# Two transformer layers on one core: the token parts of the delta rule's front made for all chunks while the membranes run, and kept in DRAM

## The chip, the cores and the metric

The kernel runs on one core of a Trainium2 chip. The metric is the device time of one execution in microseconds (us). Before the change the median of three runs is 1696.33 us (1694.0 to 1699.62). The profile comes from one execution of its own, which took 1701.06 us; its span, from the first to the last instruction, is 1699.3 us. Engines are named PE (TensorE, matmuls), PEld (its weight loads), ACT (ScalarE), DVE (VectorE), POOL (GpSimd) and SP (SyncE, which here only issues DMAs).

## The reference, cut to what matters

The input x is one sequence of 2048 tokens of width 128. The first layer normalises and modulates x and then runs a gated delta rule whose gates depend on spikes. Only this part is touched:

```
h = silu(causal_conv(rms(x)))                         # [T, 128]
q, k = unit(h @ Wq), unit(h @ Wk)                     # 8 heads of 64, each divided by its norm + 1e-6
v = h @ Wv
drive = h @ Wspike
alpha_base = silu(h @ Wau + bau) @ Wad + bad
beta_base  = h @ Wbeta + bbeta
for each token t:
    mem   = 0.9 * mem + drive[t]
    spike = mem > 0.5 ;  mem = mem - 0.5 * spike
    alpha = sigmoid(alpha_base[t] + asp * spike)      # 1 where a head has no spike
    beta  = sigmoid(beta_base[t] + sum(spike * bsp))  # 0 where a head has no spike
    s = alpha * s                                     # s: 64 x 64 per head
    s = s + (beta * k[t]) outer (v[t] - k[t] @ s)
    out[t] = q[t] @ s
```

q, k, v, alpha_base and beta_base depend on the token alone. The spikes need the membrane recurrence, and alpha, beta and the state need the spikes. After this come an output projection with a gate, a gated feed forward net, and a second layer; nothing of those is changed.

## The kernel before, in words

All data are float32. The 2048 tokens are 16 chunks (NT) of 128 (P); 8 heads are 4 pairs (NP). Four phases follow one another, each one block of code in which every engine has its own written order of instructions and waits on semaphores of the others. A phase ends when all its engines have ended. The count of a semaphore is worked out from lists of step names (`Steps`): `at(name, i)` is that step of round i, `before(name, i)` the same step one round earlier.

1. `setup_phase` (lines 76 to 329) loads weights, makes h (called `hh`, features on partitions) and the drive.
2. `spike_phase` (332 to 409) runs the membranes. DVE goes through 128 token positions, for all chunks side by side, with four small instructions for each (lines 378, 381, 383 and 385, two halves of 32 columns), and repeats the whole pass at least three times, until the states at the chunks' borders agree. Beside it PE turns x and h in 32 transposes (357) and ACT copies them back (365). Both are then done with the phase.
3. `delta_phase` (412 to 1203) works chunk by chunk. Its *back* is the delta rule of chunk i: products within blocks of 8 tokens (`base`, 767), products of neighbouring blocks of 8, 16, 32 and 64 (`blocks`, 795; the two heads of a pair stand in different halves of the rows), a row by row inversion on DVE (1102, 1107) that starts from a spread made by PE (787) and copied by ACT (618), a table `tt` (1123), transposes of it (806), four rounds of `join` (823, 834, 836, then 844, 850), and the state (858 to 888). Its *front* prepares chunk i + 1 and is woven between: projections `k`, `q`, `v`, `au` and `drive_a`, norms (sums over a head by a matmul with `bd`, then four ACT instructions and a product on DVE), the gates (`zb`, whose first half is alpha's and second beta's exponent), their running sum `G`, exponentials of its differences (`EX`, ACT line 588), and scaled copies of k and q (1033, 1039, 1047). Chunks 0 to 14 run in hardware loops; chunk 15 stands by itself, with no front.
4. `post_phase` does the rest, from about 1205 us on.

PE's order in a chunk is: `base`, `front_au` (of i + 1), `blocks`, `front_sums` (i + 1: 4 matmuls for `drive_a`, 2 of 512 columns for the norms, 8 for beta), `transposed`, `join` 8, `front_count` (i + 1, 512 columns), `join` 16 and 32, `last_join`, `state1`, `solve`, `front_late` (v of i + 1), `seen_by_q`, `front_k` and `front_q` (of i + 2), `state2`. Each matmul of this program is two MATMUL records in the trace.

DVE's order is: `front_spikes` (967, and 969 for au), `base`, `front_au` (974, 976, 978), `blocks` with `tt`, `front_z`, `front_sums`, the joins with `front_active` and `front_exponents` between them, `rest`, `front_unit`, `keep` (1152), `front_upper`, `update` (1157), `front_late`.

POOL squares k and q (511), multiplies spikes (513), and scales beta k (517, 521).

Of the kernel before, what the change touches and what calls it, by code (L numbers as in the profile page):

```python
# [19 lines left out]
P = 128  # L20
# [55 lines left out]
def setup_phase(nc, m, a):  # L76


    with ExitStack() as ctx:
# [164 lines left out]
        def _(eng):  # L244
            eng.memset(m.eps[:, 0:1], 1e-5)
            eng.memset(m.eps[:, 1:2], 1e-6).then_inc(vector_done, vec.one("eps"))
# [84 lines left out]

def spike_phase(nc, m):
# [6 lines left out]
    with ExitStack() as ctx:  # L339
# [9 lines left out]
        turned = ctx.enter_context(nc.semaphore("rows_turned"))  # L349
        columns = ctx.enter_context(nc.semaphore("columns_kept"))  # L350

        @block.tensor
        def _(eng):
            for k in range(8):
                src = (m.x, m.h)[k // 4]
                for n in range(4):
                    ins = eng.transpose(m.ps[:, k, P * n:P * n + P], src[:, 4 * (k % 4) + n, :], m.ident[:, :])
                ins.then_inc(turned, 1)

        @block.scalar  # L360
        def _(eng):
            for k in range(8):
                dst = (m.x, m.h)[k // 4]
                eng.wait_ge(turned, k + 1)
                eng.activation(dst[:, 4 * (k % 4):4 * (k % 4) + 4, :].rearrange("p n d -> p (n d)"), m.ps[:, k, :], ACT.Copy).then_inc(columns, 1)
# [46 lines left out]
def delta_phase(nc, m):  # L412
# [11 lines left out]
    with ExitStack() as ctx:  # L424
# [17 lines left out]
            "tensor_front": "k q au drive_a ksum qsum beta count v",  # L442
            "scalar_front": "hh k q au_e zb_e zb_ln beta_e n_ln n_rt n_ln2 n_rec lift_p lift_n v lift_up lift_all last",
            "vector_front": "spikes au0 au1 au2 au z b1 guard zfloor b0 active log_a G mid"
            + "".join(f" lo{s} hi{s}" for s in UPPER) + " toend unit b3 beta_k kq_base"
            + "".join(f" kq{s}" for s in UPPER) + " kq_all k_end",
            "pool_front": "square push km_base" + "".join(f" km{s}" for s in UPPER),
# [10 lines left out]
        beta_bias = ctx.enter_context(nc.semaphore("beta_bias"))  # L458
# [8 lines left out]
        square = m.arena[:, 4608:5632]  # L467
# [34 lines left out]

        @block.gpsimd
        def _(eng):
            eng.sem_inc(pool_front, fpool.credit)

            def front(n):

                eng.wait_ge(scalar_front, fact.at("q", n))
                eng.wait_ge(tensor_front, fpe.before("qsum", n))  # L510
                eng.tensor_tensor(square, kqf, kqf, ALU.mult).then_inc(pool_front, fpool.one("square"))
# [20 lines left out]
        def _(eng):  # L532
# [4 lines left out]
            def front_tokens(n):  # L537
                eng.wait_ge(tensor_front, fpe.before("v", n))
                eng.activation(m.hh_tile[:, :], m.hh[:, tok(n)], ACT.Copy).then_inc(scalar_front, fact.one("hh"))

            def front_kq(n):
                eng.wait_ge(tensor_front, fpe.at("k", n))
                eng.wait_ge(vector_front, fvec.before("kq_all", n))
                eng.wait_ge(pool_front, fpool.before("square", n))
                eng.activation(kq[:, 0, :], m.ps[:, 4, :], ACT.Copy).then_inc(scalar_front, fact.one("k"))
                eng.wait_ge(tensor_front, fpe.at("q", n))
                eng.activation(kq[:, 1, :], m.ps[:, 5, :], ACT.Copy).then_inc(scalar_front, fact.one("q"))  # L547

            def front_au(n):
                eng.wait_ge(vector_front, fvec.at("au0", n))  # L550
                eng.activation(m.au_e[:, :], m.au_x[:, :], ACT.Exp, scale=-1.0).then_inc(scalar_front, fact.one("au_e"))

# [11 lines left out]

            def front_norm1(n):

                eng.wait_ge(vector_front, fvec.at("guard", n))
                eng.activation(m.norm[:, :], m.norm[:, :], ACT.Ln).then_inc(scalar_front, fact.one("n_ln"))

            def front_norm2(n):  # L570
                eng.wait_ge(scalar_front, fact.at("n_ln", n))
                eng.activation(m.norm[:, :], m.norm[:, :], ACT.Exp, scale=0.5).then_inc(scalar_front, fact.one("n_rt"))

            def front_norm3(n):
                eng.wait_ge(scalar_front, fact.at("n_rt", n))
                eng.activation(m.norm[:, :], m.norm[:, :], ACT.Ln, bias=m.eps[:, 1:2]).then_inc(scalar_front, fact.one("n_ln2"))
                eng.wait_ge(scalar_front, fact.at("n_ln2", n))
                eng.activation(m.norm[:, :], m.norm[:, :], ACT.Exp, scale=-1.0).then_inc(scalar_front, fact.one("n_rec"))
# [17 lines left out]

            def front_v(n):
                eng.wait_ge(tensor_front, fpe.at("v", n))
                eng.wait_ge(vector_back, vec.before("rest", n))
                eng.activation(m.v[:, :], m.ps[:, 3, :], ACT.Copy).then_inc(scalar_front, fact.one("v"))  # L600
# [59 lines left out]
            front_tokens(0)  # L660
            front_kq(0)
            front_au(0)
            front_gates(0)
# [1531 lines left out]
```

## Time and profile before

| what | value |
|---|---|
| median of three runs | 1696.33 us (1694.0 to 1699.62) |
| profiled execution, its span | 1701.06 us, 1699.3 us |
| PE, PEld, DVE, ACT, POOL busy | 1178.4, 902.6, 1103.5, 601.2, 198.3 us |
| mean granted TensorE clock | 0.795 |
| membranes (first to last pass) | 96.5 to 284.7 us |
| delta rule, 16 chunks | 290 to 1204 us |
| DMA over the span | 7.22 MB, mean 4 GB/s |

Times within a phase are us from the span's start. The granted clock is a share: 1.00 is 2.4 GHz and 0.50 is 1.2 GHz, the only two levels in this trace. The engines overlap, so their busy times do not add up to the span; what a change is worth is to be read in its own phase.

### The profile page before, as it was taken

What the parts mean: (1) busy time and instruction counts of PE and PEld (TensorE: products, weight loads), DVE (VectorE), ACT (ScalarE), POOL (GpSimd) and SP (SyncE); (2) the same over time, 40 slices, a digit from 0 to 9 for tenths busy, and PEclk for the clock granted to TensorE, in tenths of its full rate; (3) what the DMA queues carried; (4) which work ended last, traced back from release to release, by engine and by line L of the source; (5) the groups of instructions that cost most, each with busy time, mean ns of one, the idle gap of its engine ahead of it and who ended that gap; (6) DMA issues with size and microseconds to landing.
All of it is one profiled execution on the core that took longest, in us unless ns stands there. A gap on an engine that the chain in (4) does not pass through costs nothing. (4 is left out here: it accounts for less than half of the span.)

```text
span 1699.3 us, 25028 instructions
## 1 busy us (share of the span) xinstructions
PE 1178.4 (69%) x8364; PEld 902.6 (53%) x8364; DVE 1103.5 (65%) x3471; ACT 601.2 (35%) x935; POOL 198.3 (12%) x189
## 2 busy tenths in 40 slices
PE   1230001488888988898888988889666879688786
PEld 1110001377777877787777876779423526346272
DVE  4788988777887778877797777872133325343251
ACT  3120000333444334443444534441325355363422
POOL 2000001301211012110211102110010102001000
PEclk8575555688899889898988999895578788886966
DMA  2000000000000000000000000000200000000000
GB/s 72 0 1 1 1 1 1 1 1 0 0 0 0 0 0 0 0 0 0 0 0 0 0 0 0 0 1 1 58 0 1 0 0 8 0 7 1 0 8 6
DMA packets 9746, 7.22 MB, mean 4 GB/s; under 512 B 3158, under 2 KB 7831, under 8 KB 9690
## 3 DMA queue, kind: packets, MB, share of 16 engines
q1 hardware_dynamic: 8170, 5.07, 1.1%
q10 hardware_dynamic: 1520, 1.48, 0.3%
q8 instruction: 25, 0.41, 0.1%
q14 instruction: 31, 0.25, 0.1%
HBM read 5.50 MB, written 1.05 MB: 4 GB/s over the span
## 5 line engine op out<-in xcount | busy, mean ns | idle before, releaser
L1133 DVE TENSOR_TENSOR delta_tm<-delta_tm,ps 128x256 f32<-128x256 f32 x96 | 40.4, 421 | 156.7 <-PE ps L836 156.7
L795 PE MATMUL ps<-delta_kq_up,delta_arena 64*128 64x128 f32 x1024 | 111.2, 400 | 37.2 <-ACT delta_kq L547 36.5
L795 PEld LDWEIGHTS ps<-delta_kq_up,delta_arena 64*128 64x128 f32 x1024 | 102.4, 302 | 62.2 <-ACT delta_kq L547 37.4
L893 PE MATMUL ps<-ones,beta_b 1*128 1x1 f32 x8 | 1.8, 346 | 190.9 <-PEq L339 190.9
L633 ACT ACTIVATE delta_xf<-ps 128x256 f32<-128x256 f32 (+1 forms) x128 | 48.9, 382 | 204.5 <-PE ps L823 140.2
L517 POOL TENSOR_TENSOR delta_km<-delta_beta_k,delta_arena 128x512 f32<-128x512 f32 x16 | 32.6, 2037 | 635.9 <-DVE delta_beta_k L1030 635.9
L834 PE MATMUL ps<-delta_xf,delta_tt 128*128 128x64 f32 x768 | 106.6, 284 | 0.0
L836 PE MATMUL ps<-delta_tt,delta_xf 128*128 128x64 f32 x768 | 106.6, 284 | 0.0
L823 PEld LDWEIGHTS ps<-delta_tm,drive 128*128 128x128 f32 x768 | 95.6, 201 | 17.0 <-DVE delta_zb L984 9.1
L893 PEld LDWEIGHTS ps<-ones,beta_b 1*128 1x128 f32 x8 | 1.8, 322 | 191.1 <-issue 191.1
L823 PE MATMUL ps<-delta_tm,drive 128*128 128x64 f32 x768 | 98.5, 284 | 6.1 <-ACT delta_tm L623 6.1
L834 PEld LDWEIGHTS ps<-delta_xf,delta_tt 128*128 128x128 f32 x768 | 98.6, 201 | 0.0
L836 PEld LDWEIGHTS ps<-delta_tt,delta_xf 128*128 128x128 f32 x768 | 98.6, 201 | 0.0
L378 DVE SCALAR_TENSOR_TENSOR kept<-mem 128x32 f32<-128x32 f32 x384 | 73.3, 191 | 12.3 <-remote 11.2
L1039 DVE TENSOR_TENSOR delta_kq_up<-delta_kq,delta_arena 128x256 f32<-128x256 f32 x128 | 75.8, 651 | 1.4
L383 DVE SCALAR_TENSOR_TENSOR mem<-kept,drive 128x32 f32<-128x32 f32 x384 | 73.3, 191 | 0.0
L385 DVE SCALAR_TENSOR_TENSOR mem<-kept,drive 128x32 f32<-128x32 f32 x384 | 71.7, 187 | 0.0
L381 DVE SCALAR_TENSOR_TENSOR kept<-mem 128x32 f32<-128x32 f32 x384 | 71.6, 187 | 0.0
L533 ACT ACT_TABLE_LOAD x1 | 1.3, 1283 | 189.5 <-PEq L339 189.5
L521 POOL TENSOR_TENSOR delta_arena<-delta_beta_k,delta_arena 128x256 f32<-128x256 f32 x64 | 57.2, 923 | 6.3 <-ACT delta_arena L588 6.3
L787 PE MATMUL ps<-drive,delta_block_ones 128*128 128x512 f32 x32 | 29.3, 1015 | 39.4 <-DVE drive L1070 37.4
L767 PE MATMUL ps<-delta_kq_base,delta_km 64*128 64x256 f32 x256 | 37.7, 417 | 25.2 <-DVE delta_state L1157 14.2
(372 smaller groups left out, 2923.1 us busy)
## 6 DMA issues: line engine op xcount, KB each, us to landing
out<-post_rows SPq DMA_DIRECT2D x4, 256.0 KB, 2.3
setup_wmod<-in_L_wmod ACTq DMA_DIRECT2D x2, 384.0 KB, 3.4
post_wff<-in_L_attn_Wff SPq DMA_DIRECT2D x3, 256.0 KB
post_w<-in_L_ffn_w SPq DMA_DIRECT2D x2, 256.0 KB
post_fc_q<-in_L_ffn_fc_q SPq DMA_DIRECT2D x2, 256.0 KB
setup_wspike<-in_L_attn_Wspike ACTq DMA_DIRECT2D x1, 256.0 KB
wq<-in_L_attn_Wq ACTq DMA_DIRECT2D x1, 256.0 KB
wk<-in_L_attn_Wk SPq DMA_DIRECT2D x1, 256.0 KB
```

Source lines behind the costliest of these rows:

```text
L378: eng.scalar_tensor_tensor(m.kept[:, a_half], u[:, t, a_half], 1.0, u[:, t, a_half], ALU.is_gt, ALU.subtract).then_inc(step_a, 1)
L381: eng.scalar_tensor_tensor(m.kept[:, b_half], u[:, t, b_half], 1.0, u[:, t, b_half], ALU.is_gt, ALU.subtract).then_inc(step_b, 1)
L383: eng.scalar_tensor_tensor(u[:, t + 1, a_half], m.kept[:, a_half], -DECAY, d[:, t, a_half], ALU.mult, ALU.add).then_inc(step_a, 1)
L385: eng.scalar_tensor_tensor(u[:, t + 1, b_half], m.kept[:, b_half], -DECAY, d[:, t, b_half], ALU.mult, ALU.add).then_inc(step_b, 1)
L521: eng.tensor_tensor(lo, halves(m.beta_k[:, :], s)[:, :, 0, :], lo, ALU.mult).then_inc(pool_front, fpool.one(f"km{s}"))
L633: eng.activation(dst, src, ACT.Copy).then_inc(scalar_back, act.one(f"X{s}{x}"))
L795: ins = eng.matmul(m.ps[:, at + h % 2, P * (h // 2):P * (h // 2) + P], up_lift[s][ks, cs], m.kq_up[s][ks, :, half], start=True, stop=True)
L823: ins = eng.matmul(m.ps[:, 4 + n, HD * (h % 4):HD * (h % 4) + HD], bt[s][:, h, :], cols(m.tm[:, h, :], 0), start=True, stop=True)
L834: eng.matmul(m.ps[:, 6 + n, HD * (h % 4):HD * (h % 4) + HD], m.tt[:, h, :], cols(m.xf[:, h, :], 0), start=True, stop=True)
L836: ins = eng.matmul(m.ps[:, 6 + n, 256 + HD * (h % 4):256 + HD * (h % 4) + HD], m.xf[:, h, :], cols(m.tt[:, h, :], 1), start=True, stop=True)
L1039: ins = eng.tensor_tensor(m.kq_up[s][:, a, :].rearrange("p (b s) -> p b s", s=s), halves(kq[:, a, :], s)[:, :, 1, :], halves(up_lift[s], s ...
L1133: eng.tensor_tensor(v, v, m.ps[:, 6 + n, 0:256].rearrange("p (b s) -> p b s", s=s), ALU.subtract).then_inc(vector_back, vec.one(f"TX{x}{s}"))
```

## The change

`prepare`, called in the spike phase in place of the bare transposes, makes k, q (with their norms), v, alpha_base and beta_base of all 16 chunks in 4 groups of 512 tokens and writes them to three DRAM tensors. PE has 28 matmuls of 512 columns for a group, ACT 13 instructions of 2048 columns and 4 of 512, POOL two products of 2048 columns, and SP five stores of 1 MB. Before them stand the old transposes and copies, the biases, and au of all tokens (4 matmuls; ACT copy, Exp, Ln, Exp; two POOL instructions). SP ends the phase by waiting for all stores.

In the delta phase SP loads each chunk's `zb`, `kq` and `v` into the same single buffers as before, each as soon as chunk i's last reader is done. The steps `hh`, `k`, `q`, `au_e`, the four norms and `v` leave ACT; `k`, `q`, `au`, `drive_a`, `ksum`, `qsum`, `v` and half of `beta` leave PE; `au0`, `au1`, `au2`, `au`, `guard` and `unit` leave DVE; `square` leaves POOL. With them go the waits on those steps. `front_z` and `b1` now add to what was loaded.

```diff
+def prepare(nc, ctx, m, block):          # called by spike_phase
+    @block.tensor
...
+        def projected(g, which, w, b):
+            for c in range(NP):
+                ins = eng.matmul(m.ps[:, 4 * b + c, :], w[:, c * P:c * P + P], m.hh[:, group(g)], start=True, stop=True)
...
+        for g in range(NG):
+            eng.wait_ge(scalar_made, act_at("b", g - 1) if g else act0.at("turn7"))
+            projected(g, "k", m.wk, 0)
+            eng.wait_ge(scalar_made, act_at("q_ln", g - 1) if g else act0.at("au"))
...         # v, then ksum, q, z, qsum, b
+    @block.scalar
...
+        for g in range(NG):
+            kept(g, "k", 0)              # copy, Square
...         # v copy
+            normed(g, "k", 0)            # Ln, Exp, Ln, Exp
+            kept(g, "q", 1)
...         # z copy, four b
+            normed(g, "q", 1)
+    @block.gpsimd
+        eng.memset(m.au[R:R + 1, :], 1.0).then_inc(pool_made, pool0.one("ones"))
+        eng.wait_ge(scalar_made, act0.at("au"))
+        eng.tensor_scalar(m.au[0:R, :], m.au[0:R, :], FLOOR, None, ALU.max).then_inc(pool_made, pool0.one("floor"))
+        eng.wait_ge(scalar_made, act0.at("au_sig"))
+        eng.tensor_tensor(m.au[0:R, :], m.au[0:R, :], m.au_e[:, :], ALU.mult).then_inc(pool_made, pool0.one("silu"))
+        for g in range(NG):
+            for a, which in enumerate("kq"):
+                eng.wait_ge(scalar_made, act_at(f"{which}_rec", g))
...
+                eng.tensor_tensor(by_chunk(m.unit[:, a, :]), by_block(m.raw[:, a, :]), by_block(m.norms[:, :]), ALU.mult).then_inc(pool_made, pool.one(which))
...
+        @block.sync                      # delta phase
+            def scores_and_gates(n):
+                if n:
+                    eng.wait_ge(vector_front, fvec.at("G", n - 1))
+                    eng.wait_ge(scalar_front, fact.at("beta_e", n - 1))
+                eng.dma_start(zb[:, :, :], m.zb_store[n]).then_inc(zb_in, 16)
...         # values(n) after "rest", keys_and_queries(n) after "kq_all" of chunk n - 1
         def chunk(i):
             base(i)
             eng.wait_ge(scalar_back, act.before("out", i))
-            front_au(i + 1)
-            blocks(i, True)
-            front_sums(i + 1)
+            blocks(i)
+            front_beta(i + 1)            # 4 matmuls of 128 columns
             transposed(i)
             join(i, 8)
             front_count(i + 1)
...
             solve(i)
-            front_late(i + 1)
             seen_by_q(i)
-            if not last:
-                eng.wait_ge(scalar_back, act.at("kend", i))
-                front_k(i + 2)
             eng.wait_ge(scalar_back, act.at("solved", i))
-            if not last:
-                front_q(i + 2)
             state2(i)
```

## Rows read from the trace of the kernel before

**Rows 1.** The page: busy time of the engines, and granted clock in 40 slices.
```profile
PE 1178.4 (69%) x8364; PEld 902.6 (53%) x8364; DVE 1103.5 (65%) x3471; ACT 601.2 (35%) x935; POOL 198.3 (12%) x189
PEclk8575555688899889898988999895578788886966
```

**Rows 2.** Windows: stretch, length, busy PE, PEld, DVE, ACT, POOL, clock, DMA share, GB/s.
```profile
96.50:284.70 188.20, 2.91 (x27) 2.67 (x25) 176.38 (x1551) 3.92 (x8) 0.00 (x0) 0.52 0.00 1
709.90:712.30 2.40, 0.08 (x1) 0.00 (x0) 2.40 (x5) 1.07 (x2) 0.00 (x0) 0.69 0.00 0
718.10:723.90 5.80, 5.77 (x35) 4.04 (x35) 5.46 (x20) 1.67 (x5) 0.00 (x0) 0.50 0.00 0
723.90:728.50 4.60, 4.60 (x29) 3.64 (x28) 4.19 (x15) 0.65 (x2) 0.00 (x0) 0.94 0.00 0
728.10:754.90 26.80, 25.94 (x230) 24.86 (x229) 16.68 (x35) 12.88 (x23) 0.00 (x0) 1.00 0.00 0
758.70:781.80 23.10, 17.41 (x145) 13.21 (x144) 22.18 (x63) 6.75 (x16) 6.48 (x6) 0.78 0.00 0
```

**Rows 3.** Windows of chunk 15, which has no front.
```profile
1145.00:1150.80 5.80, 5.76 (x34) 3.99 (x34) 4.13 (x20) 1.67 (x5) 0.00 (x0) 0.50 0.00 0
1150.80:1154.10 3.30, 0.00 (x0) 0.00 (x0) 3.16 (x10) 0.65 (x2) 0.00 (x0) 0.95 0.00 0
1154.10:1200.00 45.90, 45.83 (x222) 45.03 (x224) 5.66 (x15) 5.64 (x14) 0.00 (x0) 0.50 0.00 1
```

**Rows 4.** Timeline of a middle chunk: start, us, engine, line, operation.
```profile
712.14 0.33 DVE L969 TENSOR_SCALAR delta_au_x<-ps,bau 64x128 f32<-64x128 f32 x1
718.13 2.07 PE L787 MATMUL ps<-drive,delta_block_ones 128*128 128x512 f32 x2 [1.98 <-DVE drive L1070]
720.24 0.60 ACT L618 ACTIVATE drive<-ps 128x512 f32<-128x512 f32 x1 [7.43 <-PE ps L787]
726.88 1.23 DVE L1123 TENSOR_TENSOR delta_tt<-drive,delta_block_of 128x1024 f32<-128x1024 f32 x1
735.48 1.08 PE L746 MATMUL ps<-delta_spk,bd 128*128 128x512 f32 x2
752.86 1.99 PE L869 MATMUL ps<-drive,delta_tt 128*128 128x64 f32 x16 [0.44 <-DVE drive L1146]
754.89 0.60 ACT L650 ACTIVATE delta_u_rows<-ps 128x512 f32<-128x512 f32 x1
756.38 2.33 ACT L588 ACTIVATE delta_arena<-delta_arena 128x2560 f32<-128x2560 f32 x1
```

**Rows 5.** Timeline of chunk 15.
```profile
1147.74 0.17 DVE L1102 TENSOR_TENSOR drive<-drive 128x8 f32<-128x8 f32 x1 [1.53 <-ACT drive L618]
1152.89 1.22 DVE L1123 TENSOR_TENSOR delta_tt<-drive,delta_block_of 128x1024 f32<-128x1024 f32 x1
1196.25 3.68 PE L869 MATMUL ps<-drive,delta_tt 128*128 128x64 f32 x16
```

**Rows 6.** Lines 1152 and 181: count, duration ns min/median/max, first and last start.
```profile
L1152 DVE TENSOR_TENSOR delta_state<-delta_state,delta_last x16: 426/1499/1516, 382.5 to 1201.9; 128x256 f32<-128x256 f32 x16
L181 ACT ACTIVATE setup_arena<-setup_arena x1: 1909/1909/1909, 14.2 to 14.2; 128x2048 f32<-128x2048 f32 x1
```

**Rows 7.** Timeline of POOL and DVE.
```profile
712.48 1.89 POOL L511 TENSOR_TENSOR delta_arena<-delta_kq 128x1024 f32<-128x1024 f32 x1 [3.80 <-ACT delta_kq L547]
756.33 2.03 POOL L517 TENSOR_TENSOR delta_km<-delta_beta_k,delta_arena 128x512 f32<-128x512 f32 x1 [40.96 <-DVE delta_beta_k L1030]
757.14 1.50 DVE L1152 TENSOR_TENSOR delta_state<-delta_state,delta_last 128x256 f32<-128x256 f32 x1
766.18 1.89 POOL L511 TENSOR_TENSOR delta_arena<-delta_kq 128x1024 f32<-128x1024 f32 x1 [3.80 <-ACT delta_kq L547]
```

**Rows 8.** Timeline of the first chunk's front.
```profile
315.35 1.06 ACT L556 ACTIVATE delta_zb<-delta_zb 128x1024 f32<-128x1024 f32 x1 [12.43 <-DVE delta_zb L990]
323.89 2.32 ACT L588 ACTIVATE delta_arena<-delta_arena 128x2560 f32<-128x2560 f32 x1
```

More of the change, by code:

```diff
@@ L329, in _, with prepare_tensors, sb @@
                                           2.0, None, ALU.mult).then_inc(vector_done, vec.one(f"drive{n}"))
+def prepare_tensors(nc, ctx, m):
+    def sb(name, shape, dt=F32):
+        return ctx.enter_context(nc.sbuf_tensor("prep_" + name, shape, dt))
+    m.raw = sb("raw", [P, 2, 2048]); m.squares = sb("squares", [P, 2048]); m.norms = sb("norms", [P, 2048])
+    m.unit = sb("unit", [P, 2, 2048]); m.v_rows = sb("v_rows", [P, 2048]); m.zb_cols = sb("zb_cols", [P, 2, 2048])
+    m.au = sb("au", [R + 1, T]); m.au_e = sb("au_e", [R, T]); m.beta_bias = sb("beta_bias", [P, NP])
@@ L348, in spike_phase @@
         a_half, b_half = slice(0, W), slice(W, 2 * W)
[L349 to L365, printed above, removed]
+        prepare(nc, ctx, m, block)
         @block.vector
@@ L441, in delta_phase @@
             + " rest keep update",
[L442 to L445, printed above, removed]
+            "tensor_front": "beta count",
+            "scalar_front": "zb_e zb_ln beta_e lift_p lift_n lift_up lift_all last",
+            "vector_front": "spikes z b1 zfloor b0 active log_a G mid"
+            + "".join(f" lo{s} hi{s}" for s in UPPER) + " toend b3 beta_k kq_base"
             + "".join(f" kq{s}" for s in UPPER) + " kq_all k_end",
-            "pool_front": "square push km_base" + "".join(f" km{s}" for s in UPPER),
+            "pool_front": "push km_base" + "".join(f" km{s}" for s in UPPER),
         }
@@ L535, in _ @@
             eng.sem_inc(scalar_back, act.credit)
[L537 to L551, printed above, removed]
             def front_gates(n):
@@ L713, in head, with front_beta @@
                 return slice(HD * (h % 2), HD * (h % 2) + HD), slice(P * (h // 2), P * (h // 2) + P)
-            def project(bank, w, rhs, rows=P):
+            def front_beta(n):
+                eng.wait_ge(vector_front, fvec.at("spikes", n))
+                eng.wait_ge(vector_back, vec.before("up8b", n))
                 for c in range(NP):
-                    ins = eng.matmul(m.ps[:, bank, c * P:c * P + P], w[:, c * P:c * P + P], rhs, start=True, stop=True)
-                return ins
-            def front_k(n):
-                project(4, m.wk, m.hh[:, tok(n)]).then_inc(tensor_front, fpe.one("k"))
@@ L769, in base, with blocks @@
                                 ins.then_inc(tensor_back, pe.one(f"base{n + e}"))
-            def blocks(i, ahead):
+            def blocks(i):
                 for s in UPPER:
@@ L830, in join @@
                         eng.wait_ge(vector_back, vec.at(f"up16{x}", i))
-                        if ahead:
-                            eng.wait_ge(vector_front, fvec.at("guard", i + 1))
                     for h in range(4 * n, 4 * n + 4):
@@ L890, in state2, with chunk @@
                 ins.then_inc(tensor_back, pe.one("update"))
[L892 to L905 removed]
+            front_beta(0)
+            front_count(0)
+            def chunk(i):
                 base(i)
                 eng.wait_ge(scalar_back, act.before("out", i))
[L909 to L911 removed]
+                blocks(i)
+                front_beta(i + 1)
                 transposed(i)
```

283 lines of the change are left out of this document (176 added, 107 removed).

## The prediction

> **What bounds the kernel now.** I read the page first, then windows by stretch, then the timeline of one middle chunk and of the last one. The page shows PE and DVE both near two thirds, and a granted clock that is low in slices 4 to 8 and again after the delta rule [rows 1]. The windows tell why. While the membranes run (96.5 to 284.7) DVE has 1551 instructions and PE, ACT and POOL have next to nothing [rows 2]: this is the free room the change wants. In the delta rule line 511 comes once a chunk, at 712.48 and at 766.18 [rows 7]: a chunk has a period of 53.7 us.
>
> I cut that period at three points. (A) From the end of `tt` on DVE (726.88 + 1.23 = 728.1) to the end of the solve on PE (752.86 + 1.99 = 754.85): 26.8 us, PE busy 25.9, clock 1.00. (B) From there to the end of ACT's 2560-column Exp (756.38 + 2.33 = 758.7): 3.9 us. (C) From there to the next end of `tt` (781.8): 23.1 us, DVE busy 22.2 [rows 2, 4]. So A is PE's, B is ACT's, C is DVE's, and work is worth something only where it stands on its own engine's stretch.
>
> **What leaves the loop.** Most of it is covered. On DVE the three au steps (974 to 978) are 1.4 us, but they lie under the spread: PE 2.07 and ACT 0.60 us, after which the rows may start at 720.84 [rows 4]. Chunk 15 has no au steps, and there DVE waits 1.53 us for that same copy [rows 5]. So they are worth 0. Line 969 stands in C and is worth its step of 0.3. `unit` and the four norms are on DVE and ACT in A, where PE is the bound: 0 there. In B, after the solve, ACT copies u_rows, then v (waiting for PE's v), then starts the Exp at 756.38, 0.9 after the copy of u_rows ends at 755.49; with the v step gone that 0.9 goes. On PE `front_sums` fills 723.9 to 728.5, which DVE's `tt` makes it wait for anyway until 728.1: 0.3 or so, and 0.2 more at the first join. The sum is 0.3 + 0.9 + 0.5 = 1.7 us a chunk, 15 times: 25 us, if the clock stays as it is. Bounds: 0.9 (only B) to 3 a chunk.
>
> The first chunk's front is serial and gains more. Its gates wait for au, two sums and the guard; ACT's first Exp, after 12.4 us of idle, starts at 315.35 and the 2560-column one at 323.89 [rows 8]. Without au, sums (two 512-column matmuls at half clock) and squares the first Exp can start some 11 us earlier, and the norms no longer stand between it and the last. I take 12 us (bounds 8 to 16).
>
> **What the loads cost.** Each chunk loads 1.3 MB in three transfers, each started when the chunk before has done with the buffer. Three new waits stand on DVE: on `zb` in `front_z` (behind it b1, for which PE's first join waits), on `kq` before beta k (behind it line 1033, `keep`, and PE's next `base`), on v in `rest` (behind it the solve). By the order of the code each load has most of a chunk between its start and that wait, and SP has nothing else in its queue. I take 0, with bounds of 0 and 1 us a chunk, covered by the 53.7 us of the chunk itself.
>
> **What goes under the membranes.** ACT's wide instruction is 1.91 us [rows 6], so a group of 512 tokens costs it 13 x 1.91 + 4 x 0.6 = 27 us, plus waits for ksum and for qsum and b. Four 512-column matmuls are 3.4 us at full clock, 6.8 at half (the pair of line 787 takes 2.07 at 0.50, that of line 746 1.08 at 1.00 [rows 4], about 0.2 of each being pipeline). That makes 36 to 45 us a group, 144 to 180 for four. Transposes, au and its three Exp/Ln take some 25 ahead, the last product and store some 9 behind: 178 to 214 from 96, an end at 274 to 310. The membranes end at 284.7 now.
>
> But POOL does not run beside DVE for nothing. Line 1152 reads two operands from SBUF; in chunk 15, with POOL idle, it takes 0.43 us, in the 15 others 1.50, and it ends at 758.64, right after POOL's line 517 ends at 758.36 [rows 6, 7]. DVE was held until POOL's instruction was over. Lines 378 to 385 also read two operands from SBUF, and a pass is a chain of them. POOL gets 8 products of 2048 columns; at line 511's 1.89 us for 1024 [rows 7] that is 3.8 us each, 30 us, and two more of 2048 columns for au, 8 us. If each stops the chain for its length, the membranes take 38 us more, end at 323, and hide the whole preparation. No row shows this form held, so the bounds are 0 (not held; then the late end of the preparation costs 0 to 25 instead) and 45. I take 38, nearest to line 1152.
>
> The Trainium skill, page "SBUF — State Buffer", section "SBUF: two separate sides", calls the pair of ports that DVE and POOL share an exclusive lock, held for a whole instruction, which a DVE instruction with two SBUF inputs needs when POOL reads SBUF too. By that rule the term is the full 38. Where the trace can be read (line 1152), it agrees.
>
> **What happens to TensorE's clock.** This decides the sign. Chunk 15 is the delta rule with no front, so it is a preview. There PE stands idle from 1150.8 to 1154.1, the clock falls to 0.50, and stays there from 1154.1 to 1200.0 although PE is busy 45.83 of 45.90 us [rows 3]. The joins, 64-column matmuls each behind a weight load, do not bring it back. Stretch A takes from 1154.1 to 1196.25 + 3.68 = 1199.9 there [rows 5]: 45.8 us in place of 26.8, with less in it.
>
> In a middle chunk the clock also falls, at about 711 after a short idle (0.69 in 709.9 to 712.3), and is 0.50 through the spread and `blocks`. It comes back at 724 in `front_sums` (0.94 in 723.9 to 728.5), and PE then goes into the transposes without a pause [rows 2]. After the change `front_sums` is 4 matmuls of beta, 1.7 us at half clock and 0.9 at full. `blocks` ends at 723.9 as before (it hangs on the spread), beta by 725.6 at the latest, and `tt` is ready at 728.1. PE is idle for 2.5 to 4 us just ahead of the joins, as in chunk 15. An idle of 2.4 us was enough at 709.9. So even if `blocks` and beta raise the clock, it has fallen by the first join. The only dense matmul after that is `count`, two records of 512 columns; line 787, the same shape, ran at 0.50 at 718.13 and 0.50 was still the clock until 723.9, so one does not bring it back.
>
> Price: A becomes 45.8 + `count` at half clock, 1.8 (between 1.08 and 2.07 less pipeline) = 47.6, 20.8 more than 26.8. With B and C (0.9 and 0.3 less) a chunk takes 73.3 in place of 53.7: 19.6 more, 15 times: 294 us. Bounds: -25 (clock kept) to +300.
>
> The Trainium skill, "TensorE: Matmul & The Clock Gate", section "What's actually happening", says that the throttled clock is the default and that activity releases it. By that rule a PE that is 99% busy in the joins would be at full clock shortly, and the loop would gain the 25 us. That is the second rival below; chunk 15 speaks against it.
>
> **The sum**, against the profiled execution: 1701.1 + 294 + 38 - 12 = 2021. That run is 4.7 us above the median of those shown, so 2016.
>
> **Rivals.**
> - *Beta or count relight the clock in time.* If `count` does it, only the transposes and the first join are slow: 728.1 to 735.48 [rows 4] is 7.4 of the 26.8 us, so 7.4 x 19 / 26.8 = 5.2, plus 0.9 of count and some 2 until it takes hold, less 1.2: 7 a chunk, 105 in all. 1701 + 105 + 26 - 5 = 1827. For it: in the middle chunk the clock came back after 5.8 us of unbroken work [rows 2]. Against it: that was `blocks` and the spread together; count is one matmul.
> - *The clock holds, as the rule says, and the membranes are not held by POOL.* Then -25 - 12 and the preparation ends between 274 and 310, 0 to 25 late: 1659 to 1684, faster. It decides at one place: whether PE's idle between beta and `tt` is short enough to leave the clock up. For it: clock 0.95 is still shown in the idle 1150.8 to 1154.1, the fall comes late. Against it: it was at 0.50 right after.
> - *The clock holds, but POOL holds the membranes*: 1701 - 25 - 12 + 38 - 5 = 1697, no change.
> - *The change does not hide what it says*: the preparation outlasts even the stretched membranes. At 214 us it ends at 310, ahead of 323. It only adds up to 25 where POOL holds nothing.
>
> **Chances.** Clock lost in nearly all chunks 0.79 (own range 1960 to 2050, by bounds of 0 to 45 for the membranes and 13 to 15 chunks); relit by count or in some phases of the loop only 0.11; clock held and membranes stretched 0.05; clock held and membranes free 0.05. I put the range from 1840 to 2050. A measurement of this kernel tells about 0.3% (5 us) from no change. Faster 0.07, same 0.03, slower 0.90.
>
> **What would show it.** Clock 0.50 in the windows of all joins and a chunk period near 73 us (the spacing of line 521's instructions on POOL); PE idle 2.5 to 4 us before line 806's instructions; L1133's waits for PE doubled; the membranes' passes longer only while POOL is busy, ending near 320; the first 2560-column Exp 12 us nearer to the phase's start. It would be wrong if the joins run at 1.00.

## The result, and the profile after

| | forecast | measured |
|---|---|---|
| time | 2016 us (1840 to 2050) | 1829.9 us, median of four runs (1827.6 to 1839.9) |
| ratio to before | 1.19 | 1.081, 95% interval 1.078 to 1.083 |
| start to the first `tt` | +26 us | +27.7 (352.5 to 380.2) |
| first to last `tt`, 15 periods | +294 | +104.1 (800.4 to 904.4) |
| after the last `tt` | 0 | -5.3 (546.4 to 541.1) |

Slower, as forecast, but by 134 us and not by 320, and 10 us outside the range. The forecast's last three rows add up to its 320; the measured ones to 126.5 us, the difference of the two spans (1699.3 and 1825.8). The time is lost in the loop, and the loop has two kinds of periods: thirteen of 57 to 59 us and two of 73.8 and 73.9, where before they were 53.3 to 53.7 and the last 51.4. The first and the third of these stretches also differ between runs of the same code: in six runs with this preparation the first `tt` comes at 375.9 to 381.8 us, and from the last `tt` on it is 541.1 to 547.1 us.

The page of the kernel after, as in [rows 1]:

```profile
PE 1313.4 (72%) x7956; PEld 991.0 (54%) x7956; DVE 1065.8 (58%) x3374; ACT 628.5 (34%) x869; POOL 215.9 (12%) x184
PEclk8678885577878775778787785687567879896866
```

PE has 408 matmul records fewer and is busy 135 us longer. The windows of the kernel after, columns as in [rows 2]: the membranes, then a short period in three pieces (ahead of the transposes, through the first join and `count`, from there to the next `base`), then the joins of a long period:

```profile
96.70:325.70 229.00, 128.28 (x267) 56.31 (x266) 215.99 (x1546) 127.01 (x86) 47.10 (x11) 0.75 0.25 92
492.60:499.40 6.80, 2.59 (x32) 2.28 (x29) 6.20 (x24) 1.72 (x6) 0.00 (x0) 1.00 0.00 0
499.40:513.10 13.70, 13.70 (x60) 12.27 (x58) 3.02 (x8) 3.96 (x6) 0.00 (x0) 0.50 0.00 0
513.10:537.00 23.90, 21.36 (x219) 20.24 (x218) 16.28 (x31) 10.72 (x18) 4.75 (x5) 1.00 0.10 33
673.50:724.70 51.20, 51.20 (x252) 48.71 (x254) 16.94 (x37) 12.41 (x21) 2.14 (x2) 0.50 0.04 15
```

In 492.6 to 499.4 PE is busy 2.59 of 6.80 us, where [rows 2] have it busy 4.60 of 4.60 in `front_sums`. The clock is still 1.00 there and 0.50 from 499.4, just as the transposes begin. The same in the timeline of PE (start, us, engine, line, operation, idle before), short period first, long one below the dots; 927 is the transposes, 944, 953 and 955 the joins, 878 `count`, 963 the last join, 988 the solve:

```profile
497.53 1.23 DVE L1208 TENSOR_TENSOR delta_tt<-drive,delta_block_of 128x1024 f32<-128x1024 f32 x1
498.98 1.60 PE L927 MATMUL ps<-ident,delta_tt 128*128 128x128 f32 x8 [4.21 <-DVE delta_tt L1208]
500.58 3.67 PE L944 MATMUL ps<-delta_tm,drive 128*128 128x64 f32 x16
510.87 2.02 PE L878 MATMUL ps<-delta_spk,bd 128*128 128x512 f32 x2
512.69 2.08 PE L944 MATMUL ps<-delta_tm,drive 128*128 128x64 f32 x16
514.60 1.06 PE L953 MATMUL ps<-delta_xf,delta_tt 128*128 128x64 f32 x8
529.34 1.99 PE L988 MATMUL ps<-drive,delta_tt 128*128 128x64 f32 x16 [0.44 <-DVE drive L1231]
531.86 2.33 ACT L761 ACTIVATE delta_arena<-delta_arena 128x2560 f32<-128x2560 f32 x1
...
671.94 1.23 DVE L1208 TENSOR_TENSOR delta_tt<-drive,delta_block_of 128x1024 f32<-128x1024 f32 x1
685.60 2.02 PE L878 MATMUL ps<-delta_spk,bd 128*128 128x512 f32 x2
697.55 3.62 PE L944 MATMUL ps<-delta_tm,drive 128*128 128x64 f32 x16
717.75 3.67 PE L988 MATMUL ps<-drive,delta_tt 128*128 128x64 f32 x16
721.95 2.33 ACT L761 ACTIVATE delta_arena<-delta_arena 128x2560 f32<-128x2560 f32 x1
745.85 1.23 DVE L1208 TENSOR_TENSOR delta_tt<-drive,delta_block_of 128x1024 f32<-128x1024 f32 x1
```

Up to `count` the two periods are alike: 16 matmul records of a join take 3.67 us, where 16 records of the same width take 1.99 at the full clock [rows 4]. In the short one the clock is back at 513.1, right behind `count`, and the next 944 takes 2.08 us; in the long one it is not and the same line takes 3.62. Cut as in the prediction: A is 32.6 us in the short period (498.76 to 531.33) and 48.3 in the long (673.17 to 721.42), B 2.9 in both, C 22.6 and 22.8.

The membranes: first the group of POOL's products in 96 to 326 us (busy, mean ns), below it the timeline around one of them.

```profile
L503 POOL TENSOR_TENSOR prep_unit<-prep_raw,prep_norms 128x2048 f32<-128x2048 f32 x8 | 36.2, 4520 | 125.3 <-ACT prep_norms L471 125.3
...
139.29 0.19 DVE L557 SCALAR_TENSOR_TENSOR kept<-mem 128x32 f32<-128x32 f32 x1
139.32 4.53 POOL L503 TENSOR_TENSOR prep_unit<-prep_raw,prep_norms 128x2048 f32<-128x2048 f32 x1 [13.77 <-ACT prep_norms L471]
139.40 4.50 DVE L560 SCALAR_TENSOR_TENSOR kept<-mem 128x32 f32<-128x32 f32 x1
143.82 0.18 DVE L562 SCALAR_TENSOR_TENSOR mem<-kept,drive 128x32 f32<-128x32 f32 x1
```

A membrane instruction of 0.19 us takes 4.50 when it meets a product of 4.53. The last one starts at 325.5 instead of 283.4: +42. Each of the eight products holds one membrane instruction (3.43 to 4.54 us), and so do the two POOL instructions for au. The one with two operands (4.50 us) holds for 4.54, the one with a single operand (5.40 us) for only 3.62.

The first chunk's front, against [rows 8]: from the first Exp to the 2560-column one is 8.2 us in place of 8.5, and the ACT table load that opens the phase comes 22.0 us before the latter instead of 33.9.

```profile
345.85 1.06 ACT L744 ACTIVATE delta_zb<-delta_zb 128x1024 f32<-128x1024 f32 x1 [12.43 <-DVE delta_zb L1076]
354.09 2.34 ACT L761 ACTIVATE delta_arena<-delta_arena 128x2560 f32<-128x2560 f32 x1 [2.13 <-DVE delta_arena L1106]
```

### The profile page after: what moved, and what is told of

The parts are those of the page before. It is cut to its first block and busy times, and to the rows that moved or that the text cites. A ratio compares the mean times of both kernels' runs of the same rounds, so it can differ in the third digit from the quotient of the medians.

```text
span 1825.8 us, 23689 instructions
## 1 busy us (share of the span) xinstructions
PE 1313.4 (72%) x7956; PEld 991.0 (54%) x7956; DVE 1065.8 (58%) x3374; ACT 628.5 (34%) x869; POOL 215.9 (12%) x184
## 5 line engine op out<-in xcount | busy, mean ns | idle before, releaser
L944 PEld LDWEIGHTS ps<-delta_tm,drive 128*128 128x128 f32 x768 | 132.6, 265 | 22.4 <-DVE delta_tm L1218 7.8
L953 PE MATMUL ps<-delta_xf,delta_tt 128*128 128x64 f32 x768 | 139.2, 342 | 0.0
L955 PE MATMUL ps<-delta_tt,delta_xf 128*128 128x64 f32 x768 | 139.2, 342 | 0.0
L944 PE MATMUL ps<-delta_tm,drive 128*128 128x64 f32 x768 | 134.1, 349 | 0.9 <-DVE delta_zb L1074 0.8
L955 PEld LDWEIGHTS ps<-delta_tt,delta_xf 128*128 128x128 f32 x768 | 131.0, 257 | 0.0
L953 PEld LDWEIGHTS ps<-delta_xf,delta_tt 128*128 128x128 f32 x768 | 131.0, 257 | 0.0
L557 DVE SCALAR_TENSOR_TENSOR kept<-mem 128x32 f32<-128x32 f32 x384 | 83.6, 218 | 13.6 <-remote 12.6
L560 DVE SCALAR_TENSOR_TENSOR kept<-mem 128x32 f32<-128x32 f32 x384 | 86.0, 224 | 0.0
L407 PE MATMUL ps<-prep_squares,bd 128*128 128x512 f32 x64 | 46.4, 891 | 39.4 <-ACT prep_squares L457 39.4
L927 PE MATMUL ps<-ident,delta_tt 128*128 128x128 f32 x128 | 26.2, 372 | 65.7 <-DVE delta_tt L1208 65.7
L873 PE MATMUL ps<-delta_spk,beta_s 128*128 128x128 f32 x128 | 19.5, 297 | 70.2 <-DVE delta_spk L1067 70.2
```

Source lines behind the costliest of these rows:

```text
L557: eng.scalar_tensor_tensor(m.kept[:, a_half], u[:, t, a_half], 1.0, u[:, t, a_half], ALU.is_gt, ALU.subtract).then_inc(step_a, 1)
L560: eng.scalar_tensor_tensor(m.kept[:, b_half], u[:, t, b_half], 1.0, u[:, t, b_half], ALU.is_gt, ALU.subtract).then_inc(step_b, 1)
L944: ins = eng.matmul(m.ps[:, 4 + n, HD * (h % 4):HD * (h % 4) + HD], bt[s][:, h, :], cols(m.tm[:, h, :], 0), start=True, stop=True)
L953: eng.matmul(m.ps[:, 6 + n, HD * (h % 4):HD * (h % 4) + HD], m.tt[:, h, :], cols(m.xf[:, h, :], 0), start=True, stop=True)
L955: ins = eng.matmul(m.ps[:, 6 + n, 256 + HD * (h % 4):256 + HD * (h % 4) + HD], m.xf[:, h, :], cols(m.tt[:, h, :], 1), start=True, stop=True)
```

## Experiments

All edits are to the kernel after unless it says otherwise. Ratios are to the kernel before, with 95% intervals. "Periods" are those between the 16 `tt`.

**Is it the pause ahead of the transposes?** Four dense matmuls in it:

```diff
                 front_beta(i + 1)
+                fill(4)        # 4 x eng.matmul(m.ps[:, 4, :], m.bd, m.spk as 512 columns), unused
                 transposed(i)
```


> The changed kernel with four more 512-column matmuls in each chunk's front, issued in the gap between the beta matmuls and the transposes of the unit-triangle inverse, where TensorE waits 4.2 us for VectorE's tt; their result is used by nothing. Theory (the clock): the gap is what lets the granted clock fall to 0.50 before the joins; with the gap filled it stays near 1.00 through the joins, a join matmul costs what it costs in the warm half (1.0 to 1.1 us instead of 1.9 for its eight), the period of a chunk falls from 58.1 us (73.8 in two of them) to 52 to 54, and the whole to 1725 to 1740. Rival (the loop is longer for the loads, the moved products or added waits, and the low clock is only its symptom): 1827 or, for the added matmuls, up to 15 x 0.9 = 14 us more.

1701.3 us, 1.005 (1.003 to 1.007): 129 us less for added work. Periods 52.0 to 52.3, last 50.7; the mean of a join's record is 284 to 285 ns as before the change (342 to 349 in the kernel after). The clock theory holds, and better than expected: this pause is the whole loss of the loop, which with it filled is 19 us shorter than before (781.1 for 800.4).

**Does `count` relight the clock?** Its 512 columns as eight times 64, same place, same values:

```diff
-                eng.matmul(m.ps[:, 2, :], m.bd[:, :], spk as 512 columns)
+                for c in range(8):
+                    eng.matmul(m.ps[:, 2, 64 * c:64 * c + 64], m.bd[:, :], 64 columns of spk)
```


> The changed kernel with the matmul count, one of 512 columns, cut into eight of 64 columns with the same values; it stays behind the transposes' first join. Nothing else differs. Theory (the one dense matmul count is what brings the clock back in 13 of 15 chunks, and the forecast's term A failed at that): in narrow pieces it no longer does, all 15 chunks go like the long two, period 73 to 75 us, the whole 2015 to 2045, which is the forecast for the changed kernel. Rival (the joins relight the clock, count only happens to stand there): 58 us in most chunks and 1825 to 1845.

2053.2 us, 1.210 (1.208 to 1.213), a little above the theory's 2015 to 2045. All fifteen periods are long, 75.2 to 75.7 and the last 73.8. The window of one chunk's joins in this run, and `count`'s group (busy, mean ns; two records a matmul):

```profile
459.50:510.70 51.20, 50.78 (x255) 49.65 (x256) 15.62 (x33) 11.58 (x21) 1.80 (x1) 0.50 0.05 15
L880 PE MATMUL ps<-delta_spk,bd 128*128 128x64 f32 x256 | 57.8, 421 | 0.0
```

So in the kernel after it is that one matmul that brings the clock back. This is the step at which the prediction failed. `count` made twice in a row asks why it fails in two chunks:

```diff
+                eng.matmul(m.ps[:, 2, :], ...count's operands...)
                 eng.matmul(m.ps[:, 2, :], ...).then_inc(tensor_front, fpe.one("count"))
```


> The changed kernel with the matmul count made twice in a row, behind the first join as before. Theory (it is dense columns amid the joins that bring the clock back, and one count is just enough in 13 chunks and not in the other two): with two of them every chunk is relit; no period of 73.8 us is left, all near 58 to 60 us (a second count costs 0.9 to 1.8 us a chunk), the whole 1795 to 1825. Rival (the two long chunks come from elsewhere, and a matmul more is a matmul more): 13 chunks of 59 to 60, two of 75, 1842 to 1855.

1819.6 us, 1.074 (1.072 to 1.075). No long period is left; from the second on they alternate between 60.5 and 59.1, the last is 57.7. One `count` in this place is enough in most chunks, two are in all.

**`count` ahead of the transposes**

```diff
                 front_beta(i + 1)
+                front_count(i + 1)
                 transposed(i)
                 join(i, 8)
-                front_count(i + 1)
```


> The changed kernel with the matmul count (512 columns) moved from behind the transposes to ahead of them, beside beta; nothing is added or left out. Theory (count relights the clock): count, followed without a gap by the first join, is what brings the granted clock back from 0.50 to 1.00 in the chunks of 58.1 us; without it there every chunk goes like the two long ones (73.8 us, joins at 0.50 to their end), less the 2 us that count took at the half clock: period 71 to 73 us, the whole 2005 to 2030. Rival (the relighting comes from the joins themselves and the order of one matmul is nothing): 58 us a chunk and 1820 to 1830 in all.

1754.6 us, 1.039 (1.032 to 1.046): neither theory. Twelve periods are 51.3 (49.9 to 51.7) and three in a row 72. I had thought of `count` as what repairs the clock and not of what it does to the pause: ahead of the transposes it splits it, and in most chunks the clock doesn't fall there. Where it does fall, nothing repairs it in the joins, as in the forecast.

**Dense, or only busy?** The filling as 32 matmuls of 64 columns:

```diff
+                    eng.matmul(m.ps[:, 4, 0:64], m.bd[:, :], m.spk[:, 0, 0:64], ...)   # x 32
```


> As the run with the gap filled (four added 512-column matmuls, period 52.2 us, 1701 us), but the filling is 32 matmuls of 64 columns, each like a join's matmul: about the same time of a busy TensorE at the full clock (a join's 16 take 1.95 us), far fewer columns for that time at the half clock. Theory (what holds the clock is how densely columns stream, not that TensorE is busy): the clock falls ahead of the joins as in the changed kernel; where it has fallen the filling takes 7.3 us of which 4.2 are gap: period 58 to 61 us, 74 to 77 in some, 1830 to 1950. Rival (no idle time is what holds it): 52 to 53 us a chunk and 1700 to 1715.

1740.9 us, 1.027 (1.025 to 1.030). Periods 54.6 to 55.4, last 52.8, joins at the full pace. The row is the group of a join's line in this run:

```profile
L957 PE MATMUL ps<-delta_xf,delta_tt 128*128 128x64 f32 x768 | 106.6, 284 | 0.0
```

The theory is wrong in this half. Narrow matmuls without a pause hold a clock that is up (1.00 from 536.0 us, the filling from 538.1); they don't bring back one that is down (2053 us above). I had its length wrong too: a matmul is two records, so the filling takes 7.3 us and ends 2.9 behind `tt`, which is the 2.5 us over the dense filling's 52.2.

**The other direction: the kernel before, thinned out.** Its `drive_a`, `ksum` and `qsum` work on one column and beta's token half is left out, so its output is not the reference's.

```diff
-                project(4, m.wad, m.au[:, :])
+                eng.matmul(m.ps[:, 4, 0:1], m.wad[:, 0:P], m.au[:, 0:1], ...)
...             # ksum, qsum: 1 column; beta: the spike matmuls alone; guard floor 1.0
```


> The kernel before, with the dense matmuls that stood between its block products and its transposes thinned out: drive_a, ksum and qsum work on one column, beta on the four spike matmuls alone, and the guard's floor is 1.0 so that values stay finite (the output is then not the reference's). Products, membranes and VectorE's and ScalarE's work of a chunk stay. Theory (the clock is held by those matmuls in the kernel before): the granted clock falls at its joins too, and less work makes the kernel slower: period 58 us or more instead of 53.4, the whole 1750 to 1810. Rival (less work on TensorE is less time, the clock is not tied to these matmuls): 1640 to 1696.

1921.3 us, 1.132 (1.125 to 1.138), on the theory's side and more than it said: periods alternate between 60.4 and 76.1, the last is 74.1. `count` is left as it was, and the clock is back at 1.00 behind it in the 7 short periods only. Less work makes the kernel before 13% slower. Its dense sums, which [rows 2] show in 723.9 to 728.5, are what keeps its joins at 1.00.

**POOL's hold.** Preparation stores raw k, q and the reciprocal norms; VectorE makes the product in the loop.

```diff
-                eng.tensor_tensor(m.unit, m.raw, m.norms, ALU.mult)               # POOL, 8 times
+                eng.tensor_tensor(kq[:, :, :], kq[:, :, :], m.norm[:, :, :], ALU.mult)  # DVE, front_unit
```


> The changed kernel with the product key x reciprocal norm (and query x reciprocal norm) taken out of the preparation on GpSimd, 8 instructions of 128 x 2048 and 4.5 us each, and made by VectorE in the delta loop, one instruction a chunk; two more stores a group and one more load a chunk. Theory (GpSimd's products hold VectorE's membrane steps, 8 x 4.5 us = 36 of the 42 us by which the membranes grew): the membranes end near 290 instead of 325 us, or where the last preparation ends if that is later, the loop pays 16 x 0.6 to 1.1 us of VectorE, most of it beside TensorE: 1790 to 1800 in all. Rival (the membranes grew because the projections and evictions of the preparation share PSUM and SBUF ports with them, whichever engine makes the product): membranes end at 320 or later and the whole is 1825 to 1840.

1867.6 us, 1.102 (1.100 to 1.104), slower than with POOL's products, and yet the mechanism is confirmed. The rows are the last of the four membrane lines in the kernel after, then the last two in this run, of which the first shows one of the holds for au (count, duration ns min/median/max, first and last start):

```profile
L564 DVE SCALAR_TENSOR_TENSOR mem<-kept,drive x384: 178/191/4507, 97.1 to 325.5; 128x32 f32<-128x32 f32 x192
```
```profile
L554 DVE SCALAR_TENSOR_TENSOR mem<-kept,drive x384: 183/191/3624, 96.3 to 296.5; 128x32 f32<-128x32 f32 x192
L556 DVE SCALAR_TENSOR_TENSOR mem<-kept,drive x384: 178/191/195, 96.4 to 296.6; 128x32 f32<-128x32 f32 x192
```

The membranes win 29 us, not 36, and 13 of the 42 stay. The holds account for both: without the products 33 us of holding are gone (34.5 less the eight instructions' own 0.19), and the two for au leave 7.7 (held 3.62 and 4.49). The rest is in the two idle stretches between the passes, 5.6 us each before the change, 6.9 and 5.7 after it, 8.2 and 8.9 in this run; why they grow stays open. The first `tt` comes at 352.4 instead of 380.2. A short period is 0.7 us longer, and six are long instead of two; the loop takes 971.5 us for 904.4. Had I seen only the total, I would have drawn the wrong conclusion: as long as the clock hangs on one matmul, an edit elsewhere can change how many chunks lose it. Why it is six here and two there isn't shown.

**Together.** Product on DVE, `count` ahead of the transposes and two dense matmuls behind it; then the same with three ahead of `spread`:

```diff
                 front_beta(i + 1)
+                front_count(i + 1)
+                fill(2)
                 transposed(i)
```


> Three edits together: the unit product on VectorE in the loop (it moved the loop's start from 380.2 to 352.4 us and cost 0.7 us a chunk), count ahead of the transposes (51.3 us a chunk where the clock held, 72 in three) and two 512-column matmuls more behind it in the same gap so that no chunk loses the clock. Theory (the clock and GpSimd's hold are the change's whole loss, and the parts add up): 352.4 + 15 x 52.2 (51.3, 0.7 for the product, 0.2 for the fill) + 541 after the last tt = 1676, between 1668 and 1690, under the kernel before. Rival (the clock's falls shift to some chunks by phase, as in the run with count first alone): each chunk that loses it costs 21 us, 1700 to 1760.

```diff
                         eng.wait_ge(vector_back, vec.at("base1", i))
+                        # 3 x the filling matmul, into bank 2
                         eng.wait_ge(vector_back, vec.at("spread", i))
```


> The run before this one with three more 512-column matmuls in the gap ahead of spread, where TensorE waits 5 us for VectorE: spread and the first blocks run at the half clock there (2.08 us for its two matmuls, against about 1.1 at the full clock). Theory: spread's 1.0 us goes and the 32-block products behind it run at the full clock, 0.5 to 1.5 us a chunk: 1655 to 1672. Rival (VectorE sets this stretch and spread's half clock is hidden): the same as without it.

1691.3 us, 0.998 (0.996 to 0.999), just above the theory's 1668 to 1690, and 1708.9 us, 1.008 (1.005 to 1.010), where 1655 to 1672 was forecast. Periods of 52.5 with four of 54.2 in the first, 54.6 in the second. The timeline of PE in the second shows why, with the window of its filling below:

```profile
616.30 1.16 PE L866 MATMUL ps<-delta_spk,beta_s 128*128 128x128 f32 x8
620.70 2.08 PE L871 MATMUL ps<-delta_spk,bd 128*128 128x512 f32 x2 [3.24 <-DVE delta_a_qk L1173]
622.56 3.62 PE L875 MATMUL ps<-delta_spk,bd 128*128 128x512 f32 x4
625.98 1.40 PE L927 MATMUL ps<-ident,delta_tt 128*128 128x128 f32 x8
```
```profile
619.90:626.70 6.80, 6.00 (x10) 2.80 (x11) 4.09 (x10) 0.00 (x0) 0.00 (x0) 0.50 0.00 0
```

`count` (871) waits for VectorE 3.2 us, the clock falls to 0.50 at 619.9, and the filling behind it (875) runs at the half clock, up to the transposes. The filling stands behind the wait, and the idle stretch ahead of `count` is left.

**Filling ahead of `count`, and the product in VectorE's own pause.** This cut is against the run of 1691 us. Of the next three, the first has three filling matmuls in that place, the second also three ahead of `spread`, and the third none at all:

```diff
                 front_beta(i + 1)
+                fill(2)
                 front_count(i + 1)
-                fill(2)
...
                 front_sums(i + 1)               # DVE
+                front_product(i + 1)            # the unit product, out of front_unit
```


> The three edits of the run of 1691 us with two things moved. The two filling matmuls stand ahead of count, directly behind beta: there they need no wait, while count waits for VectorE, so the filling lies wholly inside the gap. And the unit product is made by VectorE right behind the sums, where it otherwise waits 6.2 us for TensorE's first join. Theory: the product's 0.7 us and the filling's delay of the transposes both leave the path of a chunk, period 51.3 to 51.8 us (52.6 to 54.2 before these moves), 351 + 15 x 51.6 + 541 = 1666, 1660 to 1678 in all. Rival (TensorE sets the period anyway in the joins, the product was hidden already): 1685 to 1692.

> The run before this one with three filling matmuls instead of two. Theory: at the full clock the third (0.9 us) still lies in the gap of 2.7 us, at the half clock it ends after count could start; same time as with two within 5 us, or up to 15 us less if with two some chunk lost the clock. Rival: each added matmul costs its 0.9 us a chunk, 14 us more.

> The run before this one with three more 512-column matmuls ahead of spread. Where this was tried with the filling behind count, spread and the 32-block products ran at the full clock but the clock fell in the longer idle stretch behind beta, and count and its filling took 5.5 us at the half clock. Theory: with the filling directly behind beta that stretch is not idle, so the gain at spread (1.0 us, and 1.5 us of the blocks where VectorE doesn't wait for them) is kept: 5 to 15 us less than without it. Rival (VectorE sets the stretch from base to tt): no gain, or the clock is lost elsewhere, 0 to 25 us more.

> The run of 1662 us (unit product on VectorE in its gap, count ahead of the transposes, two filling matmuls ahead of count) without the filling. Theory (the filling is what keeps the clock; count alone leaves too long a pause behind beta in some chunks): 51.3 us in some chunks, 72 in others, each of these 21 us: 1680 to 1790. Rival (the product behind the sums and count ahead of the transposes are enough, the filling does nothing): 1655 to 1665.

| | us | ratio | periods |
|---|---|---|---|
| two ahead of `count` | 1662.5 | 0.979 (0.977 to 0.981) | all 51.3, last 49.2 |
| three | 1663.2 | 0.980 (0.978 to 0.983) | the same |
| three, and three ahead of `spread` | 1649.6 | 0.972 (0.970 to 0.974) | all 50.4, last 48.9 |
| none | 1727.0 | 1.018 (1.016 to 1.020) | twelve of 51.3, three of 72 |

The filling is needed (65 us, three long periods) and two are as good as three. The filling's and the product's move were not made apart, so how the 29 us below the run of 1691 us divide between them isn't shown. The third version is the best of all, 47 us under the kernel before, and the only one whose whole interval is more than 2% below it. PE's timeline in it, to be read against the one above (906 is the filling ahead of `spread`, 908 `spread`):

```profile
491.63 4.54 PE L906 MATMUL ps<-delta_spk,bd 128*128 128x512 f32 x6 [2.22 <-DVE delta_a_qk L1153]
496.00 1.02 PE L908 MATMUL ps<-drive,delta_block_ones 128*128 128x512 f32 x2
499.94 2.74 PE L875 MATMUL ps<-delta_spk,bd 128*128 128x512 f32 x6
503.34 1.13 PE L871 MATMUL ps<-delta_spk,bd 128*128 128x512 f32 x2 [0.66 <-DVE delta_a_qk L1175]
505.15 1.09 PE L927 MATMUL ps<-ident,delta_tt 128*128 128x128 f32 x8 [0.68 <-DVE delta_tt L1212]
```

**Would the kernel before have gained the same?** It alone, with the three ahead of `spread`, and nothing else:

> The kernel before with three added 512-column matmuls ahead of spread, nothing else: is what the filling gives there a gain of the changed kernel's version, or one that the kernel before can have as well? Theory: spread goes from 2.07 us to 1.1, up to 1.0 us a chunk of the 53.4, the whole 1680 to 1696. Rival (the clock that rises early falls later, in another idle stretch): 1696 to 1720.

1852.5 us, between 1803 and 1909 in four runs, so no ratio is given; all four are slower, by 6 to 13%. The rows are PE's last pause ahead of the transposes and the first join in two chunks in a row, and the windows of the one's clock at 1.00 and of the other's joins:

```profile
520.10 1.09 PE L809 MATMUL ps<-ident,delta_tt 128*128 128x128 f32 x8 [1.43 <-DVE delta_tt L1126]
521.61 1.99 PE L826 MATMUL ps<-delta_tm,drive 128*128 128x64 f32 x16 [0.42 <-ACT delta_tm L623]
...
573.42 1.09 PE L809 MATMUL ps<-ident,delta_tt 128*128 128x128 f32 x8 [1.42 <-DVE delta_tt L1126]
574.93 3.02 PE L826 MATMUL ps<-delta_tm,drive 128*128 128x64 f32 x16 [0.42 <-ACT delta_tm L623]
```
```profile
507.40:558.60 51.20, 45.28 (x398) 38.25 (x398) 40.16 (x94) 23.05 (x40) 6.52 (x6) 1.00 0.00 0
575.70:623.50 47.80, 47.80 (x225) 44.65 (x226) 16.19 (x33) 13.73 (x23) 2.02 (x1) 0.50 0.00 0
```

The same matmuls in the same order with the same pause of 1.4 us: the first chunk keeps the clock and the second loses it, and its `count` doesn't bring it back (periods of 53.3 and 75). The rival of that expectation is right in kind, with a price beyond its 1720. The run also shows that "count always repairs it" would be as wrong as my "never": here it did so in 2 of 8 chunks.

## Why the prediction was wrong

- **A, failed.** "The only dense matmul after that is `count` ... so one does not bring it back." It does, in 13 of 15 chunks: A is 32.6 us in these and 48.3 in the two others, where 47.6 was forecast for all. The forecast's 294 us for the loop measured 104.1. The clock's share in it, 20.8 us a chunk or 312, measured 123 (904.4 us, and 781.1 with the pause filled). The run with `count` in narrow pieces is the kernel that I forecast; it takes 2053 us, for 2016. Two readings misled me. Chunk 15 [rows 3] has no `count`, so the preview had left out just what decided. And line 787 says nothing against `count`. In [rows 3] the clock is 0.50 in 1145.0 to 1150.8, through the spread and `blocks`, and 0.95 in the idle stretch behind them. That is a rise, which I read as "the fall comes late". The kernel after does the same behind the same two, though the spread (908) stands behind a pause of 5.04 us:

```profile
488.78 2.08 PE L908 MATMUL ps<-drive,delta_block_ones 128*128 128x512 f32 x2 [5.04 <-DVE drive L1155]
490.79 2.89 PE L916 MATMUL ps<-delta_kq_up,delta_arena 64*128 64x128 f32 x32
493.61 1.16 PE L873 MATMUL ps<-delta_spk,beta_s 128*128 128x128 f32 x8
...
480.30:492.60 12.30, 7.25 (x56) 5.30 (x56) 10.65 (x31) 0.60 (x1) 1.04 (x1) 0.64 0.13 43
```

From 492.6 it is 1.00 (see the windows under the result), 1.7 us after the spread ends. That the clock is still 0.50 just behind a dense matmul doesn't show that it fails to come back. Whether the spread or `blocks` brings it back there was not tested.
- **The rival "beta or count relight the clock"** gave 7 us a chunk, 105 in all, and 1827 us. Measured: 104.1 and 1829.9. Its 7 is right only as a mean, of 4.8 us in the short periods and 20.5 in the long. That the totals agree within 3 us is partly luck: it assumed one kind of chunk, and its sum is 4 us high for the profiled run (131 for 126.5). Its chance of 0.11 was too low: what spoke against it was one row, misread.
- **That the clock falls ahead of the joins**, right. PE's pause is 4.2 us, just above the forecast 2.5 to 4. That this pause is the cause is shown from both sides (filled 1701 us; made in the kernel before, 1921).
- **B and C, right:** 2.9 and 22.6 to 22.8 us, forecast 3.0 and 22.8. **The gain of the loop with the clock up:** forecast 1.7 us a chunk; with the pause filled it is 1.3 (19.3 over 15 periods), with `count` moved instead 2.1 (51.3 for 53.4).
- **Membranes, right:** +42 for 38. A product takes 4.5 us and not 3.8. Measured are 33 us of holding by the products, 7.8 by the two for au, and 1.4 of longer pauses between passes. Other runs of the same code have +38 to +43. By the Trainium skill, "SBUF — State Buffer", section "SBUF: two separate sides", POOL's instruction has the shared ports for its whole length. The trace agrees for the products (4.50 beside 4.53 us), and not for the POOL instruction with one operand (3.62 beside 5.40).
- **First front, right:** -12.0 for -12. From its last Exp to the first `tt` another 2.5 us went (28.6 to 26.1), which was not forecast; +42.1, -12.0 and -2.5 make the +27.7. **Loads, right:** no engine waits for a transfer in 385 to 1280 us. **Preparation, hidden, right:** its last product starts at 282.5 us and ends at 287.0, and the store behind it takes some 4 us, within the 274 to 310. ACT has 14 instructions of 2048 columns a group and not 13, 8 us more in all; and 2.07 less 0.2 for the pair of line 787 gives 7.5 us for four matmuls at the half clock, not 6.8. Nothing hung on either.
- The 5 us after the last `tt` were not forecast. They lie in the last phase (495.0 to 488.0 us in its window, PE 367.9 to 361.7 busy, clock 0.78 to 0.79), whose code is the same. They don't belong to the change: with `count` made twice it is 547.1 us from the last `tt` on, with the pause filled 541.6, and 546.4 before.
- The Trainium skill, "TensorE: Matmul & The Clock Gate", section "What's actually happening": activity releases the throttle. Read as in the prediction, with "activity" as PE busy, the measurement disagrees (50.78 of 51.20 us busy, clock 0.50 to the end).

## What to carry to other kernels

Before taking dense matmuls out of a loop, look at what holds the granted clock there: work that PE seems to do for nothing, in a wait for VectorE, can be worth 20 us a chunk. When a stretch without the moved work serves as a preview, list what else it lacks, and look at the clock's windows in order of time before calling a level a fall. And when a loop has periods of two kinds, take the ratio apart into their number and their length before judging an edit; a filling goes ahead of the wait, where a third matmul cost nothing here, not behind it.

## What of the hardware was unexpected

- Holding and regaining the clock are different things. Matmuls of 64 columns, put in the place of the pause, held it (periods of 54.7 us, joins of 284 ns a record) and did not regain it in 51 us of unbroken joins. A single dense matmul of 512 columns amid them did in 13 of 15 chunks of the kernel after, but in 9 of 15 with the product on DVE, 7 of 15 in the thinned kernel before, and 2 of 8 in the one with added filling; a pair did in 15 of 15.
- The same code with the same pause went either way in neighbouring chunks (1.00, then 0.50). Something besides the order of PE's work and this pause decides; these runs don't show what.
- The kernel before has its clock at 1.00 in the joins of chunks 0 to 14, yet small edits took it away: three added matmuls made it 6 to 13% slower, thinned sums 13%.
